# Reordering the start of the first attention: bias rows and router constants in later slots, first row maxima ahead of the roundings

## The reference, cut to what matters

```python
x = x + attn(layernorm(x))            # 16 heads of 64, causal, bias on q, k and v
#   q, k, v = x Wq + bq, x Wk + bk, x Wv + bv
#   att = softmax(where(causal, -inf, q k^T / 8)) / 8
#   out = (att v) proj
x = x + ffn0(layernorm(x))            # base + low-rank adapters of ranks 1, 2, 4, 8
#   proj = l2norm(x Wp + bp); simn = l2norm(sim, axis=0)
#   logits = proj simn * exp(min(temp, 4.6)); lw = softmax(logits); top 1 kept
x = x + attn1(layernorm(x))           # distance attention, 16 heads of 8
x = x + moe(layernorm(x))             # shared expert + top 2 of 8 experts
```

## Time and profile before

| | |
|---|---|
| median of 3 runs | 1182.9 us (1182.59 to 1183.47) |
| the profiled execution | 1174.82 us |
| its span, first to last instruction | 1173.0 us |
| PE busy | 1071.4 us, 91% |
| DVE, ACT, POOL busy | 770.1, 719.8, 541.1 us |
| mean granted clock of PE, share of full | 0.956 |

### The profile page before, as it was taken

The page is one execution under the profiler, slowest core; times in us unless marked ns, Lnnn a source line. Parts: engine busy times, 40 slices in busy tenths (PEclk is TensorE's granted clock), DMA queues, the critical chain, the costliest instruction groups (busy, mean ns, idle before and its releaser), DMA issues.

```text
span 1173.0 us, 16993 instructions
## 1 busy us (share of the span) xinstructions
PE 1071.4 (91%) x5839; PEld 584.6 (50%) x5839; DVE 770.1 (66%) x1547; ACT 719.8 (61%) x1173; POOL 541.1 (46%) x446
## 2 busy tenths in 40 slices
PE   4699999999999999999956799999999579999998
PEld 2445555455455545555536422222322258778876
DVE  5767877777787777777545322225221379999998
ACT  4345555555565565555422499998999466666663
POOL 1356666666656666666630000000000126788786
PEclk9789999999999999999976699999999879999999
DMA  4111111111111111110200000000000002112110
GB/s 123 27 26 37 43 33 37 43 32 31 44 43 26 44 43 26 37 44 20 64 0 1 3 8 12 12 12 9 10 11 10 10 0 93 58 69 76 67 54 37
DMA packets 35290, 40.30 MB, mean 34 GB/s; under 512 B 19652, under 2 KB 22484, under 8 KB 34188
## 3 DMA queue, kind: packets, MB, share of 16 engines
q1 hardware_dynamic: 35212, 39.30, 13.0%
HBM read 19.23 MB, written 1.11 MB: 17 GB/s over the span
## 4 chain that ended last, share of the span: by engine, by line
PE 59%; DVE 27%; issue 9%; SPq 1%; ACT 1%; POOL 1%; DMA 1%; DVEq 0%; ACTq 0%; POOLq 0%
PE banks L1003 10%; PE banks L400 8%; PE banks L991 6%; PE banks L345 5%; PE banks L385 5%; DVE qb L1308 5%; PE banks L321 5%; PE banks L386 4%; PE banks L421 3%; PE banks L366 3%; DVE kb L581 2%; DVE banks L601 2%; DVE qa L581 2%; DVE zz L630 2%; DVE qb L610 2%
## 5 line engine op out<-in xcount | busy, mean ns | idle before, releaser
L710 POOL TENSOR_TENSOR pacc<-pacc,prob 128x1024 f32<-128x1024 f32 (+3 forms) x160 | 274.0, 1712 | 64.4 <-ACT prob L512 55.1
L1012 ACT ACTIVATE prob<-banks 128x1024 f32<-128x1024 f32 x256 | 238.7, 1094 | 22.1 <-PE banks L991 22.1
L512 ACT ACTIVATE prob<-banks 128x512 f32<-128x512 f32 (+3 forms) x384 | 167.8, 488 | 113.4 <-PE banks L386 111.8
L1341 POOL TENSOR_TENSOR ka<-prob,qb 128x512 fp32r<-128x512 f32 x108 | 165.0, 1549 | 59.6 <-ACT qb L1291 33.1
L385 PE MATMUL banks<-qa,ka 128*128 128x512 f32 (+3 forms) x384 | 150.7, 400 | 1.3 <-ACT prob L512 1.3
L400 PE MATMUL banks<-prob,v 128*64 128x512 f32 (+3 forms) x768 | 145.0, 498 | 1.0 <-POOL prob L701 1.0
L1297 ACT ACTIVATE prob<-banks,w 128x512 f32<-128x512 f32 x144 | 94.7, 687 | 71.3 <-PE banks L1259 71.3
L1003 PE MATMUL banks<-prob,v 128*32 128x512 f32 x1024 | 137.1, 608 | 0.8 <-DVE pacc L1020 0.3
L386 PE MATMUL banks<-qb,kb 72*128 72x512 f32 (+3 forms) x384 | 131.5, 350 | 0.0
L957 POOL TENSOR_TENSOR sq<-sq 64x512 f32<-64x512 f32 x8 | 8.3, 1033 | 261.3 <-DVE sq L953 261.3
L701 POOL TENSOR_SCALAR_AFFINE_SELECT prob<-prob 128x256 f32<-128x256 f32 x128 | 52.1, 407 | 147.6 <-ACT prob L512 145.9
(11 more groups left out here) (211 smaller groups left out, 1610.7 us busy)
## 6 DMA issues: line engine op xcount, KB each, us to landing
qb<-qa SPq DMA_DIRECT2D x64, 128.0 KB, 2.3
ka<-ka SPq DMA_DIRECT2D x64, 128.0 KB, 2.3
prob<-gate_rows SPq DMA_DIRECT2D x8, 1024.0 KB, 4.7
w<-in_experts SPq DMA_DIRECT2D x9, 514.0 KB, 3.5
wqkv<-in_wqkv SPq DMA_DIRECT2D x16, 193.0 KB, 2.4
x<-in_x SPq DMA_DIRECT2D x4, 256.0 KB, 4.1
zz<-pacc SPq DMA_DIRECT2D x64, 16.0 KB
wpr<-pacc SPq DMA_DIRECT2D x64, 16.0 KB
```

What stands on the lines that cost most here:

```text
L512: act.activation(pr[:, j % NRING, h, 0:wd], banks[:, h, 0:wd], ACT.Exp, scale=SCALE0).then_inc(s_exp, 1)
L710: pool.tensor_tensor(pacc[:, sbk, :, o:BLK], pacc[:, sbk, :, o:BLK], pr[:, j % NRING, :, 0:wd], ALU.add).then_inc(s_padd, 1)
L1012: act.activation(prob[:, n % NP1, :], banks[:, 2 * (n % 3):2 * (n % 3) + 2, :].rearrange("p b c -> p (b c)"), ACT.Exp, scale=2 * SCALE1).t ...
L1341: pool.tensor_tensor(act2[1][:, tb % 2, i, :], hid[:, tb % 2, i, :], act2[0][:, tb % 2, i, :], ALU.subtract).then_inc(s_hlP, 1)
```

## The change

The value bias is no longer computed ahead of unit 0. Its eight matmuls stand in slot 5 of unit 1 (bias_pe part 0, into bank 5), the scaled copy on ACT in slot 6 of unit 1, four of the other matmuls and two adds in slot 5 of unit 2, and the rest in slot 5 of unit 3. The router constants stand in slot 5 of units 4, 5 and 6 on DVE (in three parts), on PE in slot 5 of units 4 and 6, on ACT in slot 6 of unit 4; they use bank 5. In these units the product of slot 4 (pv_pe, j = 4), the first that writes bank 5, waits for them.

Unit 0 has other banks: its projections go to 0, 1, 7 and 6, and none of them waits, and its max runs lie in (2, 4, 2, 2, 6, 2, 6, 2, 6, 2). Runs 0 and 1 wait only for the rounding of q and k of the first half. On DVE the order is max 0 to 2, lo 0 and 1, max 3, lo 2 and 3. Runs 0 to 3 stand ahead of slot 0; runs 4 to 9 stand in slots 0 to 3 (4; 5 and 6; 7 and 8; 9), each behind the scores of its slot. The first projections of unit 1 and the turn of unit 0's second maxima move from slot 1 to slot 3 of unit 0, behind pv 0 and 1 and run 9, and they wait for all ten runs. Context that does not change is left out.

```diff
@@ -299,6 +299,7 @@
...
         MAX_BANK = (2, 2, 2, 6, 2, 6, 2, 6, 2, 6)
+        MAX_BANK0 = (2, 4, 2, 2, 6, 2, 6, 2, 6, 2)
@@ -306,35 +307,39 @@
...
         def qk_bank(n, i):
-            return (2, 3, 7, 6)[i] if n == 0 else (2, 3, 2, 3)[i]
+            return (0, 1, 7, 6)[i] if n == 0 else (2, 3, 2, 3)[i]
...
+        def max_bank(n, r):
+            return MAX_BANK0[r] if n == 0 else MAX_BANK[r]
...
                 if not first:
-                    pe.wait_ge(s_mx, NR * (n - 1) + 9)
-            elif i == 2 and first:
-                pe.wait_ge(s_cbe, 5)
-            elif i == 2:
+                    pe.wait_ge(s_mx, NR * (n - 1) + (9 if n > 1 else 10))
+            elif i == 2 and not first:
...
         def max_pe(pe, n, w, r):
-            if r == 0:
+            if r < 2 and n == 0:
+                pe.wait_ge(s_hi0, 2)
+            elif r == 0:
                 pe.wait_ge(s_lo0, 4 * n + 2)
+            elif r == 2 and n == 0:
+                pe.wait_ge(s_mx, 1)
...
             elif r == 3 and n == 0:
-                pe.wait_ge(s_lo0, 4)
+                pe.wait_ge(s_hi0, 3)
+                pe.wait_ge(s_mx, 3)
...
                     pe.wait_ge(s_xacc, n - 1)
-            elif r == 4 and n == 0:
-                pe.wait_ge(s_mx, 3)
@@ -342,7 +347,7 @@
...
                     hp = slice(h * DH, (h + 1) * DH)
-                    mm = pe.matmul(banks[:, MAX_BANK[r] + h, at:at + width(s, c)], qa[hp, w, h, s * P:(s + 1) * P],
+                    mm = pe.matmul(banks[:, max_bank(n, r) + h, at:at + width(s, c)], qa[hp, w, h, s * P:(s + 1) * P],
@@ -396,6 +401,12 @@
...
                 pe.wait_ge(s_zz, 2 * u)
+                if u < 4:
+                    pe.wait_ge(s_cbe, 2 * u - 1)
+                elif u == 4:
+                    pe.wait_ge(s_fca, 1)
+                elif u == 6:
+                    pe.wait_ge(s_fc, 13)
@@ -405,8 +416,6 @@
...
                 pe.wait_ge(s_nw, 2 * u + sbk)
-            else:
-                pe.wait_ge(s_fc, 13)
@@ -428,8 +437,7 @@
...
             turn_pe(pe, 0, 0, True)
-            for r in range(3, 7):
-                max_pe(pe, 0, 0, r)
+            max_pe(pe, 0, 0, 3)
@@ -438,11 +446,37 @@
...
 
+        def bias_pe(pe, part):
+            if part == 0:
+                for i in range(TB):
+                    mm = pe.matmul(banks[0:HEADS, 5, 0:D], bv2[:, :], wpr[:, i, :], start=(i == 0), stop=(i == TB - 1))
+            else:
+                pe.wait_ge(s_cbe, 2 * part - 1)
+                for t in range(4):
+                    mm = pe.matmul(banks[:, 5, t * P:(t + 1) * P], pick[:, 4 * (part - 1) + t, :], cb[:, :], start=True, stop=True)
+            mm.then_inc(s_cb, 1)
...
                 scores_pe(pe, u, w, j, first)
-                if j == 0:
+                if first and j == 0:
+                    max_pe(pe, u, w, 4)
+                    v_pe(pe, u, w, bu, 1)
+                elif first and j == 1:
+                    max_pe(pe, u, w, 5)
+                    max_pe(pe, u, w, 6)
+                elif first and j == 2:
+                    max_pe(pe, u, w, 7)
+                    max_pe(pe, u, w, 8)
+                elif first and j == 3:
+                    pv_pe(pe, u, w, 0, first)
+                    pv_pe(pe, u, w, 1, first)
+                    max_pe(pe, u, w, 9)
+                    qk_pe(pe, n, x_, bn, 0, False)
+                    qk_pe(pe, n, x_, bn, 1, False)
+                    turn_pe(pe, u, 1, first)
+                elif j == 0:
@@ -460,11 +494,7 @@
...
                     pv_pe(pe, u, w, 1, first)
-                    if first:
-                        router_const_pe(pe, 0)
                 elif j == 4:
-                    if first:
-                        router_const_pe(pe, 1)
@@ -474,6 +504,12 @@
...
                         max_pe(pe, n, x_, 1)
+                    if 1 <= u <= 3:
+                        bias_pe(pe, u - 1)
+                    elif u == 4:
+                        router_const_pe(pe, 0)
+                    elif u == 6:
+                        router_const_pe(pe, 1)
@@ -552,16 +588,24 @@
...
                     v_act(act, u, w, 1)
-                elif j == 1 and not last:
+                elif first and j == 3:
                     hi_act(act, n, x_, 0)
-                elif j == 2 and not last:
                     hi_act(act, n, x_, 1)
-                elif first and j in (3, 4):
-                    router_const_act(act, j - 3)
+                elif j == 1 and not first and not last:
+                    hi_act(act, n, x_, 0)
+                elif j == 2 and not first and not last:
+                    hi_act(act, n, x_, 1)
...
                 elif j == 6:
+                    if u == 1:
+                        act.wait_ge(s_cb, 1)
+                        act.activation(cb[:, :], banks[0:HEADS, 5, 0:D], ACT.Copy, scale=SCALE0).then_inc(s_cbe, 1)
+                    elif u == 4:
+                        router_const_act(act, 0)
                     logs_act(act, u, 0, first)
+                    if u == 4:
+                        router_const_act(act, 1)
@@ -593,11 +637,11 @@
...
                 if s >= 4 and c == 0:
-                    ins = dve.tensor_reduce(mxa[:, :, s - 4], banks[:, MAX_BANK[r]:MAX_BANK[r] + 2, 0:wd], AX.X, ALU.max)
+                    ins = dve.tensor_reduce(mxa[:, :, s - 4], banks[:, max_bank(n, r):max_bank(n, r) + 2, 0:wd], AX.X, ALU.max)
...
                     low = mxa[:, h, s - 4:s - 3] if s >= 4 else NEG
-                    sc = banks[:, MAX_BANK[r] + h, at:at + wd]
+                    sc = banks[:, max_bank(n, r) + h, at:at + wd]
@@ -636,22 +680,43 @@
...
         def attn0_dve(dve):
-            for i in range(4):
-                lo_dve(dve, 0, 0, i)
...
                 max_dve(dve, 0, r, True)
-            for r in range(3, 7):
-                max_dve(dve, 0, r, True)
+            lo_dve(dve, 0, 0, 0)
+            lo_dve(dve, 0, 0, 1)
+            max_dve(dve, 0, 3, True)
+            lo_dve(dve, 0, 0, 2)
+            lo_dve(dve, 0, 0, 3)
...
 
+        def bias_dve(dve, i):
+            dve.wait_ge(s_cb, i + 2)
+            dve.wait_ge(s_xacc, i + 2)
+            for b in range(BATCH):
+                xs = x[:, b * TB + 4 * i:b * TB + 4 * i + 4, :].rearrange("p t d -> p (t d)")
+                dve.tensor_tensor(xs, banks[:, 5, :], xs, ALU.add).then_inc(s_cbe, 1)
...
             for j in range(12):
-                if j == 0:
+                if first and j == 0:
+                    max_dve(dve, u, 4, first)
+                elif first and j == 1:
+                    max_dve(dve, u, 5, first)
+                    max_dve(dve, u, 6, first)
+                elif first and j == 2:
+                    max_dve(dve, u, 7, first)
+                    max_dve(dve, u, 8, first)
+                elif first and j == 3:
+                    max_dve(dve, u, 9, first)
+                    mrow_dve(dve, u, w)
+                    lo_dve(dve, n, x_, 0)
+                    lo_dve(dve, n, x_, 1)
+                elif j == 0:
@@ -660,12 +725,8 @@
...
                     lo_dve(dve, n, x_, 1)
-                elif first and j == 3:
-                    router_const_dve(dve, 0)
                 elif j == 4:
-                    if first:
-                        router_const_dve(dve, 1)
-                    else:
+                    if not first:
@@ -675,6 +736,10 @@
...
                         max_dve(dve, n, 1, False)
+                    if u in (2, 3):
+                        bias_dve(dve, u - 2)
+                    elif 4 <= u <= 6:
+                        router_const_dve(dve, u - 4)
@@ -742,15 +807,15 @@
...
                 pe.wait_ge(s_fw, 80)
-                pe.transpose(banks[0:PROJ, 6, 0:P], wdn[:, 0:PROJ], ident).then_inc(s_fcp, 1)
+                pe.transpose(banks[0:PROJ, 5, 0:P], wdn[:, 0:PROJ], ident).then_inc(s_fcp, 1)
...
                 pe.wait_ge(s_fca, 1)
-                pe.matmul(banks[:, 6, BLK // 2:BLK // 2 + NE0], wpT[:, :], simk[:, :], start=True, stop=True).then_inc(s_fcp, 1)
+                pe.matmul(banks[:, 5, BLK // 2:BLK // 2 + NE0], wpT[:, :], simk[:, :], start=True, stop=True).then_inc(s_fcp, 1)
...
                 act.wait_ge(s_fcp, 1)
-                act.activation(wpT[:, :], banks[0:PROJ, 6, 0:P], ACT.Copy).then_inc(s_fca, 1)
+                act.activation(wpT[:, :], banks[0:PROJ, 5, 0:P], ACT.Copy).then_inc(s_fca, 1)
@@ -760,7 +825,7 @@
...
         def router_const_dve(dve, part):
-            done = [0 if part == 0 else 4]
+            done = [(0, 4, 12)[part]]
@@ -775,6 +840,10 @@
...
                 return
+            if part == 2:
+                dve.wait_ge(s_fcp, 2)
+                step(dve.tensor_tensor(wdn[:, DOWN:DALL], banks[:, 5, BLK // 2:BLK // 2 + NE0], simn[:, 2, :], ALU.mult))
+                return
@@ -785,8 +854,6 @@
...
             step(dve.tensor_reduce(simn[:, 1, :], simq[:, :, :], AX.X, ALU.add))
-            dve.wait_ge(s_fcp, 2)
```

(20 more changed lines are left out.)

## The result

The changed kernel is slower. Over 20 executions its median is 1183.8 us (1174.1 to 1185.9), that of the kernel before, beside it, 1175.5 us (1173.3 to 1183.9); the ratio is 1.0044, interval 1.0026 to 1.0062. The forecast was 1180.0, faster by 0.25%, range 1175.8 to 1184.8, and gave slower a chance of 0.10: the direction was wrong. The times lie in three groups, about 1173 to 1177, 1179 to 1180 and 1182 to 1186 us, with 12, 3 and 5 of the 20 executions of before in them, and 2, 3 and 15 of the changed kernel. The three times of before that stood ahead of the prediction, 1182.6 to 1183.5, were among its slowest; the profiled 1174.82 was the typical one. Set against that, the forecast was 1171.9. That 1183.8 lies inside the stated range is luck: the range hung on a time of before that was 7.4 too high.

The account below looks back on a forecast made before the run. PE was taken to bound units 1 to 15, with idle pieces and half clock at the start. 9.1 - 1.6 + 2.3 - 4.5 - 2.4 = 2.9 us less: 1182.9 to 1180.0 us, range 1175.8 to 1184.8.

Parts of the forecast that it names:

- The chain of unit 0: From PE's first projection at 16.08 to the fixed point (unit 1's second max run) at 51.45, at full clock.
- the 5.65 us behind slot 4: Unit 0's end: two remainders and run 0 of unit 1 put the fixed point 5.65 us after slot 4's start.
- unit 0 after: Unit 0 at full clock: the fixed point comes at 51.45 instead of 60.53, a gain of 9.1 us.
- The clock in unit 0: Sparse PE work in unit 0 drops the clock to half for a while: 1.6 us lost, bounds 0 and 6.4.
- rival 3: Half rate lasts through unit 0: slot 4 at 52.2, fixed point 57.9 or later, 1187.2 us; chance 0.12.
- At half rate PE is then dense: Unit 0, after a 2.2 us loss at half rate: dense PE work brings the clock back.
- DVE hides the rest: Unit 0: beyond the 2.2 us, DVE's work covers what PE loses at half rate.
- The clock behind it: Behind the fixed point: without the 4.99 us router wait, the half rate after it goes too, gaining 2.3 us.
- What the bias costs later: Units 1 to 3: the moved bias matmuls stand on a full PE and cost 4.0 us.
- The small router parts: Router transpose and product on PE, moved to later units: about 0.3 and 0.2 us.
- Router part 1: Unit 5: DVE step L784 is held by POOL's addition, third maxima and projections come late; 2.4 us lost.
- Sum: Whole kernel: 9.1 - 1.6 + 2.3 - 4.5 - 2.4 = 2.9 us less.

Follow-up runs that it names:

- e4: The changed kernel with idle matmuls ahead of the layernorm's transposes and in PE's holes of unit 0: 1173.0 us, ratio 0.9957 to the kernel before.
- run 9: Not a follow-up run: the last of unit 0's ten max runs (0 to 9) in the kernel, in slot 3 in the changed kernel; no time of its own.
- e12: e6 with idle matmuls ahead of the layernorm's transposes and behind max runs 0 to 2, 4 and 5 of unit 0: 1167.8 us, ratio 0.9911 to before.
- e6: Moves alone: the changed kernel with the old order and banks of unit 0; 1171.3 us, ratio 0.9943 to the kernel before.
- e13: e4 with unit 0's max run 9 in banks 6 and 7, so unit 1's first projections don't wait for it, three idle matmuls fewer: 1166.4 us, ratio 0.9914.
- e3: The changed kernel with the router constants computed in DVE's hole ahead of the first maxima, not in units 4 to 6: 1173.8 us, ratio 0.9976 to before.
- e7: e3 with the value bias's matmuls and adds moved into holes of unit 0: 1169.7 us, ratio 0.9936 to the kernel before.
- e11: The changed kernel measured and traced once more, nothing else changed: 1183.0 us, ratio 1.0038 to the kernel before.
- e14: The changed kernel with only unit 0's max run 9 moved to banks 6 and 7, so unit 1's first projections don't wait for it: 1180.2 us, ratio 1.0016.
- e5: The kernel before with only the router constants moved, into DVE's hole ahead of the bias adds: 1165.7 us, ratio 0.9893 to the kernel before.

## Why the prediction was wrong, point by point

**The chain of unit 0** was nearly right at full rate: 35.4 forecast, 36.5 in e4 with the idle matmuls and two stretches at half rate in it; slot 4 comes 29.7 behind the first projection in the forecast, 31.1 in e4. (The terms named for the 5.65 us behind slot 4 add up to 5.3; e4 has 5.4.) But the 9.1 us that I put down to "unit 0 after" are not the order's. Moves alone give 38.2 from 44.5, and with idle matmuls the old order needs 33.2. The gain comes from the bias and the router wait leaving unit 0; the order takes some of it back, 3.3 between e4 and e12, of which up to 1.7 can be the clock.

**"The clock in unit 0: I take 1.6"** is the step that failed. It cost 43.0 - 35.4 = 7.6 us against the forecast's chain, 43.0 - 36.5 = 6.5 against e4. I had its upper bound at 6.4 (its terms add up to 6.7) and described the course as rival 3 (slot 4 at 52.2, fixed point at 57.9 or later; measured 51.78 and 59.07), but gave it 0.12. Two things were missed. Half rate can hold from the first projection on, and then the first rounding is late as well. And "At half rate PE is then dense" and "DVE hides the rest" do not hold for this order: PE waits for DVE six times between 31.8 and 54.8, and each time the clock had come back (38.0, 44.8) it was lost again (41.4, 48.3), the first time behind waits of only 0.41 and 0.58 us. In the old order PE's waits lie together, ahead of a long stretch without one (e6).

**"The clock behind it, 2.3"** gave nothing. Without the router wait half rate was to be gone, but that of unit 0 ran on: until 65.3 in the changed kernel, until 67.2 in before; from one fixed point to the next unit's (96.15 in the changed kernel) it took 37.1, before 37.02.

**What the bias costs later** was right: 4.14 against 4.0. The small router parts: 0.59 against 0.5.

**Router part 1** was right in kind: 2.3 without the clock (e13) against 2.4. The held step was the one behind L784, and the 2.63 us hole of PE cost 1.7 more at half rate; I had not asked what a hole does to the clock. The Trainium skill's rule (GPSIMD Engine Reference, 1. Specifications), contention for a DVE instruction with two SBUF inputs, agrees with it: 2.35 us beside POOL's addition, 0.29 in e3 with no POOL work.

**Sum.** The forecast was -2.9, all of it by unit 7, and there the trace has 303.38 - 296.15 = +7.2 (both are starts of mrow_dve in unit 7): 10.1 more, of which 6.0 are for the clock in unit 0 (7.6 less 1.6), 2.3 for the clock behind it, 1.7 for unit 5 and 0.1 for the rest. By the end of the span it is 10.3. The last 3.1 arose in stages that the change doesn't touch, where both traces show PE at half rate in pieces of different length; that these move because the stages begin at another time is only argued, and no run tests it. How much such stages differ is on record: from unit 15's second rows to the end the 16 traces take from 596.0 us (e13) to 602.7 (e7), though no edit touches anything there:

```profile
567.61:1163.60 595.99, 534.25 (x2976) 294.48 (x2974) 343.37 (x556) 410.91 (x558) 197.10 (x135) 0.94 0.10 27
```

```profile
565.78:1168.50 602.72, 537.49 (x2976) 293.62 (x2974) 342.83 (x556) 410.99 (x558) 197.12 (x135) 0.93 0.10 27
```

So a difference of a few us between two medians need not come from the start; the run-up and the units show the edits more surely. Both kernels spread over 10 us between executions. The Trainium skill (TensorE: Matmul & The Clock Gate, Part 1) says that the windows in which activity is watched run free of the kernel, so that the place of a transition varies from run to run. No run here shows it for one kernel: the two traces of the changed kernel (this one and e11) have their falls within 0.3 us of each other, counted from the first projection. The three traces of the new order with nothing added at the start (changed, e11, e14) all began at half rate, and e6 at full, though PE's work ahead of the projections is the same. Why most executions should fall one way for a given kernel stays open.

## What to carry to other kernels

Work that leaves a stretch where PE waits anyway and goes to one where PE is full is paid in full: look for a hole of the same engines first. The router constants in DVE's first hole (e5) brought 1.07%, the change as made lost 0.44%.

When PE's work is spread between waits for another engine, cost the stretch at half rate, not at full, and treat each hole as a chance to lose the clock (here 2.63 us in a full unit, and 0.41 and 0.58 close together). In e6 the clock came back in a dense stretch behind the waits and stayed until unit 5; in the changed order it came back twice between waits and was lost again.

Set a forecast against the spread of the executions before trusting three of them.

## What the runs showed of the hardware

The clock column of a profile says nothing ahead of the first entry of its record, here at 20.95 us: 1.00 stood beside matmuls that took 6.11 us for what takes 3.70.

The same hole of 2.62 to 2.63 us in unit 5 was followed by no half rate in one trace (e13), by 3.4 us of it in five, by 6.8 in two.

Of two DVE steps with two SBUF inputs 0.33 us apart, one that began 0.1 us ahead of POOL's addition took 0.29 and the one behind its start was held for 2.35. In before the first of the two began together with the addition (55.48) and was the one held. So a shift of 0.1 us changed which step is held, not that one is.
